# A gated cross-attention and FFN kernel: scores and key projection taken two groups ahead of the attention output

## What is computed

```python
q = layernorm(x) @ Wq.T + bq
k = ctx @ Wk.T + bk
scores = where(mask, -inf, q @ k.T)
attn = softmax(scores)
x = x + tanh(g_xattn) * ((attn @ ctx) @ Wo.T + bo)
w = (weights >= 0) * 2 - 1
f = clip((layernorm(x) @ w.T) * scale + bias, -100, 100)
out = x + tanh(g_ffn) * f
```

## Time and profile before

| | |
|---|---|
| median of 3 runs | 81.12 us (80.78 to 81.38) |
| the profiled execution | 81.27 us |
| its span in the trace | 79.5 us |
| PE busy | 69.6 us, 88% |
| DVE busy | 55.8 us, 70% |
| ACT busy | 36.7 us, 46% |
| POOL busy | 55.1 us, 69% |
| mean granted TensorE clock | 0.97 |

### The profile page before, as it was taken

One profiled execution on the slowest core, in us unless ns is written; L12 is line 12 of the kernel. 1 busy time (PEld: TensorE's weight loads), 2 busy tenths in 40 slices (PEclk: granted clock), 3 DMA queues, 4 the chain that ended last, 5 costly groups with the idle time before them and its releaser, 6 DMA issues.

```text
span 79.5 us, 1571 instructions
## 1 busy us (share of the span) xinstructions
PE 69.6 (88%) x524; PEld 65.2 (82%) x524; DVE 55.8 (70%) x163; ACT 36.7 (46%) x99; POOL 55.1 (69%) x102
## 2 busy tenths in 40 slices
PE   2999999999999999999999999999999899865000
PEld 2998998996979999989999998999899798654000
DVE  2393913997669289929965980796498459899980
ACT  0053547749194519435850955294267525330000
POOL 6005667502899708889999988999999995528930
PEclk9999999999999999999999999999999999999855
DMA  1999999980000000030003003000300210300025
GB/s 22 260 369 353 349 350 348 347 255 0 0 4 0 0 0 8 0 134 2 0 4 132 8 0 132 0 0 0 132 8 0 96 36 0 117 15 0 0 71 193
DMA packets 7713, 7.44 MB, mean 94 GB/s; under 512 B 791, under 2 KB 7450, under 8 KB 7706
## 3 DMA queue, kind: packets, MB, share of 16 engines
q1 hardware_dynamic: 7376, 7.34, 28.6%
q10 hardware_dynamic: 330, 0.01, 0.2%
HBM read 5.25 MB, written 2.10 MB: 92 GB/s over the span
## 4 chain that ended last, share of the span: by engine, by line
PE 69%; DVE 16%; ACT 5%; POOL 4%; issue 2%; POOLq 0%; ACTq 0%
PE ps_K L536 14%; PE ps_Z L536 13%; PE ps_F L536 8%; PE ps_S L598 7%; PE ps_O L617 7%; PE ps_x1T L636 6%; PE ps_xT L531 4%; PE ps_cT L531 3%; PE ps_x1T L531 3%; ACT K_sb L210 2%; DVE f_biased L439 2%; DVE out_sb L444 2%; PE ps_S L606 2%; DVE bn_x L362 2%; DVE f_last L441 1%
## 5 line engine op out<-in xcount | busy, mean ns | idle before, releaser
L405 DVE SCALAR_TENSOR_TENSOR x_sb<-ps_O,recip_p,xb_sb 128x256 f32<-128x256 f32 x14 | 6.1, 480 | 9.8 <-PE ps_O L617 9.8
L322 POOL TENSOR_TENSOR f_biased<-f_scaled,bi_g 128x256 f32<-128x256 f32 x14 | 10.0, 738 | 2.9 <-DVE f_scaled L413 2.9
L316 POOL TENSOR_TENSOR xb_sb<-x_sb,bo_g 128x256 f32<-128x256 f32 x16 | 11.4, 734 | 0.5 <-ACT bo_g L247 0.5
L200 ACT CAST cT_hi<-ps_cT 128x512 fp32r<-128x512 f32 x8 | 4.7, 586 | 13.2 <-PE ps_cT L531 13.2
L304 POOL TENSOR_SCALAR xn<-x_sb,rstd_x,off_x 128x256 f32<-128x256 f32 x16 | 9.9, 626 | 0.5
L536 PE MATMUL ps_Z<-woT_hi,cT_hi 128*128 128x256 f32 x32 | 9.7, 305 | 0.0
L536 PE MATMUL ps_K<-cT_hi,wqk_hi 128*128 128x256 f32 x32 | 9.1, 283 | 0.0
L536 PE MATMUL ps_K<-cT_hi,wqk_lo 128*128 128x256 f32 x32 | 9.0, 282 | 0.0
L536 PE MATMUL ps_K<-cT_lo,wqk_hi 128*128 128x256 f32 x32 | 9.0, 282 | 0.0
L536 PE MATMUL ps_Z<-woT_lo,cT_hi 128*128 128x256 f32 x32 | 9.0, 280 | 0.0
L536 PE MATMUL ps_Z<-woT_hi,cT_lo 128*128 128x256 f32 x32 | 9.0, 280 | 0.0
(11 more groups left out here) (126 smaller groups left out, 201.1 us busy)
## 6 DMA issues: line engine op xcount, KB each, us to landing
x_sb<-in_x_dram SPq DMA_DIRECT2D x8, 256.0 KB, 6.0
ctx_sb<-in_ctx_dram SPq DMA_DIRECT2D x8, 256.0 KB, 6.3
out_dram<-out_sb SPq DMA_DIRECT2D x7, 256.0 KB, 2.1
wq_sb<-in_L_xattn_Wq_dram SPq DMA_DIRECT2D x1, 256.0 KB, 3.1
wk_sb<-in_L_xattn_Wk_dram SPq DMA_DIRECT2D x1, 256.0 KB, 3.4
wo_sb<-in_L_xattn_Wo_dram SPq DMA_DIRECT2D x1, 256.0 KB, 4.6
w_sb<-in_L_ffn_weights_dram SPq DMA_DIRECT2D x1, 256.0 KB, 5.0
out_dram<-out_sb SPq DMA_DIRECT2D x2, 128.0 KB, 1.9
```

What stands on the lines that cost most here:

```text
L316: nc.gpsimd.tensor_tensor(xb_sb[:, r], x_sb[:, r], bo_g[:], ALU.add).then_inc(xb_done, 1)
L322: nc.gpsimd.tensor_tensor(f_biased[:, r], f_scaled[:, r], bi_g[:], ALU.add).then_inc(f_biased_done, 1)
L405: nc.vector.scalar_tensor_tensor(out=x1_sb[:, r], in0=ps_O[:, b], scalar=recip_p[:, r:r + 1], in1=xb_sb[:, r], op0=ALU.mult, op1=ALU.add). ...
```

## The change

All four lists are written in another order. PE's turn `i` is now: transposes of `p` of `i`, of `ctx` and `x` of `i+2`, of `x1` of `i-1`; S of `i+1`; Z of `i`, K of `i+2`, F of `i-1`; O of `i`. So K and S of a group are made two turns' worth earlier against O than they were (S of `i+1` and K of `i+2` before O of `i`), and the full-precision work but O stands in one piece. `cT_hi` and `cT_lo` get three buffers. `norm_x` on POOL goes three groups ahead in place of two; `stats_x` of groups 2 and 3 goes in front of `woT_lo` on DVE. On DVE `split_x1T` now precedes `stats_x1` in a turn. The diff without the hunks that only turn `g % 2` into `g % 3` for `cT`, and without the block that prepares `w_cent` (moved as it is):

```diff
@@ -42,7 +42,7 @@
-    STATS_AT = {0: (2, 3), 1: (4, 5), 2: (6,), 3: (7,)}
+    STATS_AT = {0: (4, 5), 1: (6,), 2: (7,)}
...
@@ -87,7 +87,7 @@
-        cT_hi, cT_lo = sb("cT_hi", [P, 2, DC, T], F32R), sb("cT_lo", [P, 2, DC, T], F32R)
+        cT_hi, cT_lo = sb("cT_hi", [P, 3, DC, T], F32R), sb("cT_lo", [P, 3, DC, T], F32R)
...
@@ -245,23 +245,31 @@
             nc.scalar.activation(woT_hi[:], ps_woT, ACT.Identity, scale=tanh_g[:, 0:1]).then_inc(woT_hi_ready, 1)
             act.wait_ge(ps_bo_ready, 1)
             nc.scalar.activation(bo_g[:], x1T_bank[:, 0:D], ACT.Identity, scale=tanh_g[:, 0:1]).then_inc(bo_g_ready, 1)
+            evict_cT_hi(1)
+            exp(0)
+            evict_xT(1)
+            evict_Z(0)
+            evict_K(1)
             for i in range(G - 1):
-                evict_cT_hi(i + 1)
-                exp(i)
-                if i >= 1:
-                    evict_x1T_hi(i - 1)
-                evict_xT(i + 1)
-                evict_Z(i)
                 evict_PT(i)
-                evict_K(i + 1)
+                if i + 2 < G:
+                    evict_cT_hi(i + 2)
+                    evict_xT(i + 2)
                 if i == 0:
                     act.wait_ge(ps_wT_ready, 1)
                     nc.scalar.copy(wT[:], ps_x1T).then_inc(wT_ready, 1)
+                else:
+                    evict_x1T_hi(i - 1)
+                exp(i + 1)
+                if i == 0:
                     act.wait_ge(ps_rows_ready, 1)
                     nc.scalar.activation(sc_g[:], f_bank[:, 0:D], ACT.Identity, scale=tanh_g[:, 1:2]).then_inc(sc_g_ready, 1)
                     nc.scalar.activation(bi_g[:], f_bank[:, D:2 * D], ACT.Identity, scale=tanh_g[:, 1:2]
                                          ).then_inc(bi_g_ready, 1)
-            exp(G - 1)
+                else:
+                    evict_Z(i)
+                if i + 2 < G:
+                    evict_K(i + 2)
             evict_Z(G - 1)
             evict_PT(G - 1)
             evict_x1T_hi(G - 2)
...
@@ -331,6 +340,8 @@
+            offsets_x(2)
+            norm_x(2)
...
@@ -339,10 +350,10 @@
                     pool.wait_ge(clip_ready, 2)
                 if i >= 2:
                     bias_and_clip(i - 2)
-                if i + 2 < G:
-                    if unit_of(i + 2) != unit_of(i + 1):
-                        offsets_x(unit_of(i + 2))
-                    norm_x(i + 2)
+                if i + 3 < G:
+                    if unit_of(i + 3) != unit_of(i + 2):
+                        offsets_x(unit_of(i + 3))
+                    norm_x(i + 3)
                 if i >= 1:
                     rstd_1s(i - 1)
 
...
@@ -472,6 +483,8 @@
+            stats_x(2)
+            stats_x(3)
...
@@ -481,33 +494,34 @@
             dve.wait_ge(abs_g_done, 1)
             nc.vector.tensor_scalar(clip_hi[:], abs_g[:], CLIP, None, ALU.mult).then_inc(clip_ready, 1)
             nc.vector.tensor_scalar(clip_lo[:], abs_g[:], -CLIP, None, ALU.mult).then_inc(clip_ready, 1)
+            max_of_scores(0)
+            split_cT(1)
+            dve.wait_ge(w_loaded, 16)
...
             for i in range(G - 1):
                 if i >= 1:
                     residual(i - 1)
-                max_of_scores(i)
                 if i >= 2:
                     scale_ffn_out(i - 2)
-                split_cT(i + 1)
-                if i == 0:
-                    dve.wait_ge(w_loaded, 16)
...
+                if i + 2 < G:
+                    split_cT(i + 2)
+                max_of_scores(i + 1)
                 if i >= 1:
+                    split_x1T(i - 1)
                     stats_x1(i - 1)
-                    split_x1T(i - 1)
                 for g in STATS_AT.get(i, ()):
                     stats_x(g)
                 if i >= 2:
                     final(i - 2)
             scale_ffn_out(G - 3)
-            max_of_scores(G - 1)
             residual(G - 2)
             stats_x1(G - 2)
             final(G - 3)
...
@@ -653,15 +667,17 @@
             transposes(ps_woT, wo_sb).then_inc(ps_woT_ready, 1)
             pe.wait_ge(rows_loaded, 48)
             nc.tensor.matmul(x1T_bank[:, 0:D], ones_1[:], bo_row[:], start=True, stop=True).then_inc(ps_bo_ready, 1)
+            scores(0)
+            transpose_ctx(1)
+            transpose_x(1)
+            project_Z(0)
+            project_K(1)
             for i in range(G - 1):
-                scores(i)
-                transpose_ctx(i + 1)
-                if i >= 1:
-                    transpose_x1(i - 1)
-                transpose_x(i + 1)
-                project_Z(i)
-                project_K(i + 1)
+
                 transpose_p(i)
+                if i + 2 < G:
+                    transpose_ctx(i + 2)
+                    transpose_x(i + 2)
                 if i == 0:
                     pe.wait_ge(bo_g_ready, 1)
                     pe.wait_ge(w_cent_ready, DC)
...
@@ -670,9 +686,15 @@
                     nc.tensor.matmul(f_bank[:, 0:D], ones_1[:], sc_row[:], start=True, stop=True)
                     nc.tensor.matmul(f_bank[:, D:2 * D], ones_1[:], bi_row[:], start=True, stop=True).then_inc(ps_rows_ready, 1)
                 else:
+                    transpose_x1(i - 1)
+                scores(i + 1)
+
+                if i >= 1:
+                    project_Z(i)
+                if i + 2 < G:
+                    project_K(i + 2)
+                if i >= 1:
                     ffn(i - 1)
-                if i == G - 2:
-                    scores(G - 1)
                 attend(i)
             project_Z(G - 1)
             transpose_p(G - 1)
```

More of the change, by code:

```diff
@@ L199, in evict_cT_hi @@
                 act.wait_ge(cT_prod, g + 1)
-                nc.scalar.copy(cT_hi[:, g % 2], ps_cT).then_inc(cT_hi_done, 1)
+                nc.scalar.copy(cT_hi[:, g % 3], ps_cT).then_inc(cT_hi_done, 1)
             def evict_xT(g):
@@ L379, in split_cT @@
                 dve.wait_ge(cT_hi_done, g + 1)
-                nc.vector.tensor_tensor(cT_lo[:, g % 2], ps_cT, cT_hi[:, g % 2].bitcast(F32), ALU.subtract
+                nc.vector.tensor_tensor(cT_lo[:, g % 3], ps_cT, cT_hi[:, g % 3].bitcast(F32), ALU.subtract
                                         ).then_inc(cT_lo_done, 1)
@@ L483, in _ @@
             nc.vector.tensor_scalar(clip_lo[:], abs_g[:], -CLIP, None, ALU.mult).then_inc(clip_ready, 1)
+            max_of_scores(0)
+            split_cT(1)
+            dve.wait_ge(w_loaded, 16)
+            nc.vector.tensor_scalar(w_sign2[:], w_sb[:], 0.0, 2.0, ALU.is_ge, ALU.mult).then_inc(sign2_done, 1)
+            dve.wait_ge(sign2_done, 1)
+            nc.vector.tensor_reduce(w_sum[:], w_sign2[:], AX.X, ALU.add).then_inc(w_sum_done, 1)
+            dve.wait_ge(w_sum_done, 1)
+            nc.vector.tensor_scalar(w_mean[:], w_sum[:], 1.0 / D, None, ALU.mult).then_inc(w_mean_done, 1)
+            dve.wait_ge(w_mean_done, 1)
+            for c in range(DC):
+                nc.vector.tensor_scalar(w_cent[:, c], w_sign2[:, c], w_mean[:, c:c + 1], None, ALU.subtract
+                                        ).then_inc(w_cent_ready, 1)
             for i in range(G - 1):
@@ L568, in project_K @@
                         w_hi, w_lo = (w[:, c, m * P:(m + 1) * P] for w in (wqk_hi, wqk_lo))
-                        pairs += [(w_hi, cT_hi[:, g % 2, c]), (w_hi, cT_lo[:, g % 2, c]), (w_lo, cT_hi[:, g % 2, c])]
+                        pairs += [(w_hi, cT_hi[:, g % 3, c]), (w_hi, cT_lo[:, g % 3, c]), (w_lo, cT_hi[:, g % 3, c])]
                     last = accumulate(ps_K[:, m], pairs)
@@ L580, in project_Z @@
                     for c in range(DC):
-                        c_hi, c_lo = (t[:, g % 2, c, b * P:(b + 1) * P] for t in (cT_hi, cT_lo))
+                        c_hi, c_lo = (t[:, g % 3, c, b * P:(b + 1) * P] for t in (cT_hi, cT_lo))
                         pairs += [(c_hi, woT_hi[:, c]), (c_hi, woT_lo[:, c]), (c_lo, woT_hi[:, c])]
```

## The result

| | before | after |
|---|---|---|
| median of four runs | 81.18 us (80.78 to 81.38) | 83.52 us (83.46 to 84.05) |
| ratio to before, 95% | | 1.0292 [1.0248, 1.0336] |
| profiled execution / span | 81.27 / 79.5 us | 83.5 / 81.7 us |
| PE busy | 88% | 85% |
| matmul instructions, transposes included | 524 | 524 |

The change costs 2.9%. The forecast was 84.0 us, with 0.90 on slower.

What follows compares the result with a forecast made beforehand. It took PE as the bound, running without a gap from group 2 to 7, with only waits to win or lose. split_x1T(6) moves from 68.96 to 71.85, 2.9 us, giving 84.0 us against the median runs; range 82.4 to 85.4.

Steps and rivals of the forecast that it cites:

- changes of precision: PE's turn: fewer switches between full and rounded matmuls save zero; other bound 0.5 us gained.
- head: Start of the kernel: PE's wait for norm_x(2) goes, 0.19 idle and transposes 0.66 to 0.44, together 0.4 us gained.
- stall of the x1 transposes: Turns 1 to 5: PE waits for DVE's residual, 0.2 us a turn, 1.0 us in all; bounds zero and 1.5.
- PE idle in turn 6: Only the transposes of p cover residual(5): PE idle 1.1 us; as a sign, a wait of about 0.85 for x1.
- The end: Behind O(5): late rstd_1(5) holds DVE and POOL; final(5) waits for POOL's clip; split_x1T(6) ends at 71.85, before 68.96.
- nothing is late next there: Head, after PE's wait for norm_x(2) goes: no later wait, since POOL has norm_x done a turn ahead.
- the turn: Loop, O to O: 7.4 us, against 7.20 in the chain of the kernel before.
- No loss in the loop: Rival: the x1 transposes lose nothing in the loop, giving 83.0 us; chance 0.13.
- A shorter end: Rival: split_x1T(6) doesn't wait for final(5), POOL's chain being 1 us faster; split at 70.9, 83.0 us; chance 0.10.
- Dear changes of precision: Rival: each change of precision costs more than modelled; 0.22 each would balance the 2.9 us loss; chance 0.08.
- More meetings of POOL with DVE: Rival: POOL's later start adds 0.5 per further meeting with a two-input DVE instruction; two more give 85.0 us; chance 0.12.
- The clock: Rival: PE idle from 70.4 until 71.9 drops the clock, F(6) and following work take twice as long, 85.6 us; chance 0.05.

Runs made afterwards that it cites:

- 12 more stretches: Kernel before, Z and K cut in halves with sets of transposes between, turns 1 to 6, same matmuls; ratio 0.9925, 80.67 us.
- three experiments: Changed kernel with one edit each: split_x1T(6) before final(5), 1.0228; add_bo(7) right behind add_bo(6), 1.0193; K(7) back in turn 6, S(7) behind F(5), 1.0127.
- the x1 transposes behind S: Changed kernel with the transposes of x1 of group i-1 moved behind S of group i+1 on PE; ratio 1.0178, 82.94 us.
- the two edits: Changed kernel with the x1 transposes moved behind S on PE and add_bo(7) right behind add_bo(6) on POOL; ratio 1.0074, 81.93 us.
- the kernel with the head alone: Kernel before with statistics of groups 2 and 3 ahead of woT_lo and norm_x three groups ahead, nothing else; ratio 1.0023, 81.56 us.
- K(7), S(7) late: Changed kernel with K(7) put back into turn 6 between Z(6) and F(5), and S(7) behind F(5); ratio 1.0127, 82.25 us.

## Why the prediction was right, step by step

| term | predicted | measured | where |
|---|---|---|---|
| changes of precision | 0 | 0 | 7.19 against 7.20 with 12 more stretches |
| statistics ahead of `woT_lo` | 0 | 0 | 0.63 of idle left |
| head | -0.4 | -0.75 | the -0.56 of the accounts holds turn 1's stall of +0.19 |
| stall of the x1 transposes | 5 x 0.2 | 5 x 0.19, less 4 x 0.04 | 0.63 for 0.44; Z and F shorter |
| O(5) | 60.7 | 60.15 | |
| PE idle in turn 6 | 0.85 of the 1.1 | 0.85 | the 1.1 has the slower start in it |
| O(5) to the split's end | 11.15 | 11.04 | |
| the whole | 2.9 | 2.23 profiled, 2.34 by medians | |

- **The end**, the largest term, was right in its mechanism and to 0.1 in size, and three experiments took pieces out of it near the prices on record (0.5, 0.8 and 1.3 measured; 0.4, 0.8 and 1.4 expected); a fourth, the x1 transposes behind S, took nothing, since a wait for the copy of p stood behind the one removed. The three pieces hang together: behind O(5) there is too little for PE to do, so `rstd_1(5)` comes late against PE's work, and two lists queue behind it.
- **The stall in the loop** was right in place and size; removing it alone gave 0.9.
- **Mis-sized: the head.** It was named with 0.4 and came to 0.75. 0.17 was there at the first K already (10.00, before 10.17): the four weight products in front took 0.97 for 1.14, with the same instructions. The other 0.2 is two small losses of the kernel before that the prediction passed over. By the starts in the timelines of PE, the transposes of p(0) and of `w_cent` take 0.83 there (17.39 to 18.22) and 0.21 + 0.53 = 0.74 in the changed kernel; the bias row and O(0) take 1.49 (18.76 to 20.25) and 0.53 + 0.87 = 1.40. The first is a wait for `w_cent` too short to show as idle; why O(0) is longer behind the bias row is not shown. The prediction also said that nothing is late next there. That failed: `w_cent` is late, by 0.65 for it and `w_mean` (1.44 for 0.79). It cost nothing in the changed kernel's profiled execution only because PE reaches the transposes of `w_cent` later; it cost 0.5 in that of the two edits, and all of the gain in the kernel with the head alone.
- **Mis-sized: the turn**, 7.35 and not 7.40. Z takes 1.38 in some turns and kernels and 1.41 to 1.42 in others, with the same twelve matmuls. What decides it stays open.
- **The rivals.** No loss in the loop: refuted by 0.63. A shorter end: refuted, `final(5)` is what the split waited for, and it waited 0.90 for POOL's clip. Dear changes of precision: refuted by an experiment of its own. More meetings of POOL with DVE: one was foreseen (0.54, I had 0.69), no other lay on the path.
- **The clock.** PE ran nothing from 69.70 to 71.25. Windows of the changed kernel (length, then busy time by engine, PE first, granted clock third from the end):

```profile
70.50:71.20 0.70, 0.00 (x0) 0.00 (x0) 0.70 (x3) 0.00 (x0) 0.62 (x2) 1.00 0.00 0
```

  The granted clock stayed 1.00, that is 2.4 GHz, and F(6) took 1.21 in the chain, against 1.22 before. This is the page's row of the granted clock in 40 slices, in tenths:

```profile
PEclk9999999999999999999999999999999999999955
```

  It falls only in the last two slices, behind the last matmul. At the start of an execution this row proves nothing: it shows the full clock there too, while the warm-up transposes took 0.23 each, twice the 0.11 of later ones. There durations have to be read, and the prediction misread them: between the slow and the fast transposes of the earlier trace rows stand four matmuls, so these rows don't speak against the rule of the Trainium skill, "TensorE: Matmul & The Clock Gate", Part 4, that transposes don't count as PE activity and don't bring the full clock. The trace of the kernel with the head alone does. Its 20 warm-up transposes took 3.74 in all, and the last four of them, by its timeline of PE,

```profile
4.65 0.60 PE L640 MATMUL ps_x1T<-ident 128*128 128x128 f32 x4
```

  where the last four in the kernel before took 1.06. 0.60 is what four take at full speed (last row), and PE's first matmul that is no transpose starts at 5.42, behind them. So the full clock came when nothing but transposes had run on PE, and in the loop 14 of them in a row did not bring it down.

What stays open: the size of Z, and O(0) behind the bias row. The x1 transposes behind S and K(7), S(7) late were not run together, so whether they would take back the whole 2.9% is not shown.

## What to carry to other kernels

When work is pulled ahead by a group, the matmul total stays and the loop looks nearly the same, but the last turn loses its cover: lay the lists of the other engines beside what is left behind the last full turn, and follow the one value (here the rstd) for which two lists queue. Before reordering whole stages to remove a wait, look for the one instruction that can go later by one place: moving the x transposes behind Z gave 0.8 us, where the large change lost 2.3 to 2.4. And a piece of work brought forward on POOL is not free because POOL was idle: see what DVE does in that stretch and who waits for it.

## What the runs showed of the hardware

- **DVE and POOL slow each other.** `w_cent` took 1.05 for 0.62 and `w_mean` 0.39 for 0.17 beside POOL's `xn` and `xb`; POOL's two-element `ve` took 0.54 to 0.69 beside DVE's `final`, 0.19 alone. Not every DVE instruction is slowed: `w_sum` took 0.69 beside POOL in the kernel with the head alone and 0.69 with POOL idle in the kernel before. In the last group the same DVE instruction of 128x256 took 0.97 beside POOL and 0.45 with POOL idle but for its first 0.15, from the chain of the changed kernel:

```profile
75.09 0.97 DVE f_biased L450
...
78.20 0.45 DVE f_biased L450
```

- **Alternating full-precision and rounded matmuls costs nothing measurable**: 12 more stretches, 7.19 against 7.20 us a turn.
- **Transposes that had to wait take 0.63 to 0.66 for four**, in stream 0.44, so a released set costs 0.2 more than the idle time shows. A wait too short to show as idle can cost as much: 0.19 in each turn of the changed kernel, 0.09 at the transposes of `w_cent` in the kernel before.
